# Gated delta rule with a routed feed-forward: the sums of squares of the output move to ScalarE's accumulator

## The chip, the core and the metric

The kernel runs on one core of a Trainium2 chip, as one launch. The metric is the device time in microseconds (us). The kernel before takes 2626.98 us, the median of three runs (2621.15 to 2629.7). Below, PE is TensorE, DVE is VectorE, ACT is ScalarE, POOL is GpSimd, and SP is the engine that only issues transfers.

## What is computed

The reference adds three things: the input x, a routed feed-forward of layernorm(x) (the best 2 of 8 experts for each token), and an attention of the gated delta rule on layernorm(x). There are 4 sequences of 2048 tokens, 256 channels, 8 heads, keys of 128 and values of 64. Cut to the part that matters here, all in float32:

```python
def step(S, inp):                       # over the tokens of a sequence
    q_t, k_t, v_t, g_t, b_t = inp
    S = S * jnp.exp(g_t)[..., None, None]
    u = (v_t - jnp.einsum('bhk,bhkv->bhv', k_t, S)) * b_t[..., None]
    S = S + jnp.einsum('bhk,bhv->bhkv', k_t, u)
    o_t = jnp.einsum('bhk,bhkv->bhv', q_t, S)
    return (S, o_t)
...
o = gated_delta_rule(q, k, v, g, beta)
gv = (x @ Wg).reshape(Bx, Tx, H, DV)
o = o * lax.rsqrt(jnp.mean(o * o, axis=-1, keepdims=True) + EPS) * norm_w
o = o * jax.nn.silu(gv)
return o.reshape(Bx, Tx, H * DV) @ Wo
```

The change is about `jnp.mean(o * o, axis=-1)`: for each token and head, the sum of the squares of 64 numbers.

## The kernel before, in words

There are three stages, one after the other: `norm_and_route` (layernorm, routing), `experts` (the feed-forward) and `attention`. Only `attention` is changed. Every engine runs its own list of instructions, written out in the program by hand, strictly in that order; semaphores (`wait(engine, name, count)`, `then_inc`) connect the lists. There is no scheduler, so an instruction that waits holds up all that stands behind it on its engine.

`attention` handles the 4 sequences side by side as 4 lanes of 32 partitions. The 2048 tokens of a sequence are 16 groups (the variable m) of 4 chunks (c) of 32 tokens. So a chunk is 128 rows, 32 tokens of each lane, and there are 64 chunks in all. For each group an engine runs two pieces:

- `scan(m, par, f)`: the four chunks of group m in order. With S the state of all heads, a chunk is this chain: PE `read_keys` (keys times S), DVE `read` (scales it into `ks`) and `residual` (`R`), PE `solve`, ACT `spread` (copies the result into `W`), PE `apply_state` in two halves, and DVE `apply_state` in two halves, which writes the new S. Only then can the next chunk's `read_keys` begin. Beside the chain PE makes `read_queries` and `apply_scores`, ACT copies them into `t2` (`read`), DVE adds them into the chunk's output `O` (`apply_scores`, L1670). Then comes the norm of the output: POOL squares it (`squares`, L1889, into `osq`, which is the same memory as `ks`), DVE sums 64 squares per head (`squares_sum`, L1690, into `ss`), POOL makes the factor (`factor`, L1896 and L1899: an addition and a power -1/2), and DVE scales by the factor and by the gate in the next chunk's list (`scale_out`, L1695 and L1699). PE turns the result (`turn`, L1233) and ACT copies it out (`turn`, L1452 into `oT`).
- `after_keys(f, ...)`: everything of the next group f = m + 1 that must be there before its scan: the projections and short convolutions of its values and queries, and on DVE `invert`, a chain of 69 small dependent steps that inverts the 32x32 triangles.

The keys of the next group are made inside the scan of this one, one pair of heads for each chunk: PE `project_head(f, c, h)`, ACT `tap3_head(f, c, h)` (a small copy into `tails`, L1366, and the first product of the convolution into `cv`, L1369), DVE `head_taps` (a small correction, L1543, which waits for `tap3_done`, and three taps, L1548), and ACT `silu(f, other, c)` (L1381 into `kT`), after which `cv` goes on. In the scan of ACT the order in a chunk is: `tap3_head(f, c, 0)`, `spread`, `tokens`, `tap3_head(f, c, 1)`, in chunk 0 `decays` (an exponential, with a table load), `read`, `tokens`, `turn(m, c - 1)`, `silu(f, other, c)`. In chunk 0 of a group with a next one a second table load stands ahead of `silu`. In the scan of DVE it is: `read`, `residual`, the correction of the next keys, taps with `expert_rows` and `scale_out(m, c - 1)` between them, `apply_state(m, c, 0)`, and after more taps `apply_state(m, c, 1)` and `squares_sum(m, c)`; in chunk 3 `squares_sum` stands ahead of `apply_state(m, c, 1)`. In after_keys PE begins with `keys(f, par, 0)`, which needs `silu(f, other, 3)`, and DVE begins `invert` after its two products L1600, the second of which needs `keys(f, par, 1)`.

The functions that are changed, and those that call them:

Of the kernel before, what the change touches and what calls it, by code (L numbers as in the profile page):

```python
# [12 lines left out]
ALU = mybir.AluOpType  # L13
# [6 lines left out]
P = 128  # L20
# [819 lines left out]
def attention(nc, keep, dims, loaded_params, NPARAM, xf, xnT_d, yg_d, stat_d, of):  # L840
# [11 lines left out]
    with ExitStack() as ctx:  # L852
        def sb(name, shape, dt=F32):
# [15 lines left out]
        Y = sb("Y", [P, U, CT]); AT = sb("AT", [P, 2, U, CT])  # L869
        lanes = sb("lanes", [P, CT, CT]); lane_t = sb("lane_t", [P, 256]); vr = sb("vr", [P, GROUP, HV]); ktok = sb("ktok", [P, 2, H, P])  # L870
        S = sb("S", [P, LANES, HV]); Sd = sb("Sd", [P, LANES, HV])
        ks = sb("ks", [P, HV])[:, :]; osq = ks
        R = sb("R", [P, HV]); W = sb("W", [P, H, 2, DV]); in_pair = sb("in_pair", [P, 2])
        t2 = sb("t2", [P, HV]); O = sb("O", [P, HV]); O3 = sb("O3", [P, HV])
        ss = sb("ss", [P, H]); f1 = sb("f1", [P, H]); fo = sb("fo", [P, H])
# [9 lines left out]
        names = {  # L885
            "tensor": "proj_ready gate_ready norms_mm dexp_ready kk_ready qk_ready vtr_ready ktok_ready "
                      "ks_ready s_read w_ready aw_ready sup_ready otr_ready wo_ready",
            "scalar": "tap3_done tails_done silu_done sq_ready gate_done dec_done ktok_done w_spread t2_done oT_done vr_done",
            "vector": "tap taps_done norm_read nq_done nk_done kk_used qk_used elim "
                      "ks_scaled r_done o_sum s_half s_done ss_done o2_done o3_done acc1_done acc2_done fin_done",  # L890
            "gpsimd": "wt_done sidx_done k_halo_step k_halo vq_halo_step vq_halo qg_ready knorm_done "
                      "sd_half sd_done osq_done f_step f_done",
        }
        s = {n: ctx.enter_context(nc.semaphore("att_" + n)) for group in names.values() for n in group.split()}
        consts = ctx.enter_context(nc.semaphore("att_consts"))
# [68 lines left out]
        def heads(ap):  # L964

            return ap.rearrange("p (h v) -> p h v", h=H)
# [375 lines left out]
        def _(act):  # L1342
# [80 lines left out]
            def read(m, par, c):  # L1423
# [5 lines left out]
                    last = A(t2[:, DV * h:DV * h + DV], pC[:, 1, DV * h:DV * h + DV], ACT.Copy, scale=mst[:, par, c, 2, h:h + 1])  # L1429
                last.then_inc(s["t2_done"], 1)  # L1430

            def spread(m, c):

                n = GROUP * m + c
                wait(act, "w_ready", n + 1)
                for two in range(2):
                    wait(act, "sup_ready", 2 * n - 1 + two)
                    if two == 0:
                        wait(act, "aw_ready", n)
                    hs = slice(4 * two, 4 * two + 4)  # L1440
                    for k in range(2):
                        last = A(W[:, hs, k, :], heads(pC[:, 0, :])[:, hs, :], ACT.Copy, scale=in_pair[:, k:k + 1])  # L1442
                    last.then_inc(s["w_spread"], 1)
# [55 lines left out]
            def scan(m, par, f):  # L1499
                more = f is not None  # L1500
                other = 1 - par
                for c in range(GROUP):
                    if c == 0:
                        read(m, par, 0)
                    if more:
                        tap3_head(f, c, 0)
                    spread(m, c)
                    if c in (1, 2):
                        tokens(m, par, c + 1, 0)
                    if more:  # L1510
                        tap3_head(f, c, 1)
                    if more and c == 0:
                        decays(f, other, 0)
                    if c:
                        read(m, par, c)
                    if c in (1, 2):
                        tokens(m, par, c + 1, 1)
                    if c:
                        turn(m, c - 1)
                    if more:  # L1520
                        silu(f, other, c)
                    if more and c == 3:
                        decays(f, other, 1)
                if more:
                    after_keys(f, other, m)
                else:
                    turn(m, 3)
# [4 lines left out]
        def _(dve):  # L1532
# [108 lines left out]
            def read(m, par, c):  # L1641
                n = GROUP * m + c
                wait(dve, "ks_ready", n + 1)
                wait(dve, "ss_done", n)
                dve.wait_ge(mst_loaded, 16 * m + 16)
                wait(dve, "r_done", n)
                V.tensor_tensor(heads(ks), heads(pC[:, 0, :]), bc(mst[:, par, c, 2, :], 2, DV), op=ALU.mult).then_inc(s["ks_scaled"], 1)
# [33 lines left out]
            def expert_rows_2(m, c):  # L1681
                n = GROUP * m + c
                wait(dve, "acc1_done", n + 1)
                V.scalar_tensor_tensor(out=xr[:, c, :], in0=yb[:, c, 1, :], scalar=wt[:, c, 1:2], in1=xr[:, c, :], op0=ALU.mult, op1=ALU.add).then_inc(s["acc2_done"], 1)

            def squares_sum(m, c):
                n = GROUP * m + c
                wait(dve, "osq_done", n + 1)
                wait(dve, "f_done", n)
                V.tensor_reduce(ss[:, :], heads(osq), op=ALU.add, axis=AX_X).then_inc(s["ss_done"], 1)  # L1690

            def scale_out(m, c):
                n = GROUP * m + c
# [55 lines left out]
            def scan(m, par, f):  # L1749
                more = f is not None  # L1750
                for c in range(GROUP):
# [29 lines left out]
                        pass  # L1781
                    for _ in fill_late:
                        pass
                    if c == 3:
                        squares_sum(m, c)
                    apply_state(m, c, 1)
                    if c < 3:
                        squares_sum(m, c)
                    if c == 3:
                        expert_rows(m, c)  # L1790
                        expert_rows_2(m, c)
# [10 lines left out]
        def _(pool):  # L1802
# [79 lines left out]
                G.tensor_tensor(new, old, bc(mst[:, par, c, 4:4 + LANES, hs], 3, DV),  # L1882
                                op=ALU.mult).then_inc(s["sd_done" if two else "sd_half"], 1)

            def squares(m, c):
                n = GROUP * m + c
                wait(G, "o_sum", n + 1)
                wait(G, "ss_done", n)
                G.tensor_tensor(osq, O[:, :], O[:, :], op=ALU.mult).then_inc(s["osq_done"], 1)  # L1889

            def factor(m, c):

                n = GROUP * m + c
# [20 lines left out]
            def scan(m, par, f, last):  # L1914
                more = f is not None
                for c in range(GROUP):
                    if more and c == 0:
                        decay_sums(f, 1 - par, 0)
                    if c < 3:
                        read(m, par, c + 1, 0)  # L1920
                    squares(m, c)
                    if more and c == 2:
                        decay_sums(f, 1 - par, 1)
                    if c < 3:
# [36 lines left out]
```

## Time and profile before

| | |
|---|---|
| median of three runs | 2626.98 us |
| the profiled execution | 2646.84 us, of it the span 2645.2 us |
| busy, share of the span | PE 82%, DVE 72%, ACT 49%, POOL 42% |
| the granted clock of PE, mean over the span | 0.978 of full speed |
| a group of the attention, 1011 to 1116 us | PE 91.39, DVE 96.12, ACT 64.73, POOL 45.51 us busy of 105 |

The span begins with routing and experts (about 830 us, in which PE reaches 9 tenths only in the experts) and goes on with the attention's groups, each some 105 to 110 us long: about 48 us of scan and 57 us of after_keys. A timeline row gives the start and the duration in us, the engine (PEld is PE's loading of weights), the line, the operation, what is written from what, the shapes, and in brackets the idle time of the engine before it with what ended it. Small numbers can overlap: on one engine an instruction may start about 0.1 us before the one ahead of it is done. A group of rows of the view by line gives count, busy time, mean duration of one, and the idle time before them.

### The profile page before, as it was taken

The numbers are of one execution on the slowest core, as the hardware profiler recorded it, in microseconds if no ns is written. First come the engines' busy times: TensorE is split into PE (matmuls) and PEld (weight loads), VectorE is DVE, ScalarE is ACT, GpSimd is POOL, SyncE is SP. The second block draws the span as 40 slices with busy tenths as digits, with TensorE's granted clock in tenths as the row PEclk, the third lists the DMA queues.
The fourth block names the chain that finished last, engine by engine and source line by source line (L and its number), as shares of the span: only waits on it lengthen the run. The fifth ranks groups of instructions, "written<-read, shape, count | busy, mean of one in ns | idle before, by whom it ended". The sixth has DMA issues, their size and how long they took to land. (4 is left out here: it accounts for less than half of the span.)

```text
span 2645.2 us, 93006 instructions
## 1 busy us (share of the span) xinstructions
PE 2173.0 (82%) x36317; PEld 1501.1 (57%) x36318; DVE 1896.5 (72%) x3928; ACT 1302.6 (49%) x3667; POOL 1120.0 (42%) x1123
## 2 busy tenths in 40 slices
PE   3222399999997798988989889898888988989886
PEld 2222399999995364555645546455464555645555
DVE  5343352223222789998898998989989999899985
ACT  0000144444433656566565665656656566565662
POOL 3444344444443242634426344263442634526333
PEclk9999999999998899999999999999999999999998
DMA  6445122222222101001010010100101001010000
GB/s 200 155 154 182 49 71 70 70 75 72 74 70 76 35 4 44 22 25 31 16 43 23 25 32 15 44 23 25 32 15 44 23 25 33 15 44 23 25 22 23
DMA packets 106778, 135.23 MB, mean 51 GB/s; under 512 B 39584, under 2 KB 80064, under 8 KB 106176
## 3 DMA queue, kind: packets, MB, share of 16 engines
q0 software_dynamic: 23296, 60.85, 7.4%
q1 hardware_dynamic: 65952, 48.91, 6.7%
q10 hardware_dynamic: 17184, 20.49, 2.3%
q8 instruction: 261, 4.28, 0.7%
q14 instruction: 85, 0.70, 0.1%
HBM read 76.18 MB, written 54.00 MB: 49 GB/s over the span
## 5 line engine op out<-in xcount | busy, mean ns | idle before, releaser
L1548 DVE SCALAR_TENSOR_TENSOR att_cv<-att_psA,att_cw,att_cv 128x508 f32<-128x508 f32 (+2 forms) x660 | 480.0, 739 | 7.6
L1085 PE MATMUL att_psA<-att_xt,att_wqkv 128*128 128x512 f32 x880 | 445.1, 640 | 14.1 <-DMA att_xt<-xn_cols 12.7
L1882 POOL TENSOR_TENSOR att_Sd<-att_S,att_mst 128x1024 f32<-128x1024 f32 x128 | 242.9, 1903 | 461.7 <-DVE att_S L1662 438.6
L807 PE MATMUL moe_psHT<-moe_xT,moe_w1s 128*128 128x128 f32 x2176 | 268.0, 277 | 0.3 <-issue 0.3
L1085 PEld LDWEIGHTS att_psA<-att_xt,att_wqkv 128*128 128x128 f32 x880 | 161.1, 199 | 184.0 <-issue 167.7
L817 PE MATMUL moe_psY<-moe_w,moe_hT 128*128 x1088 | 258.1, 380 | 0.0
L807 PEld LDWEIGHTS moe_psHT<-moe_xT,moe_w1s 128*128 128x128 f32 x2176 | 256.1, 193 | 0.9 <-issue 0.5
L672 ACT ACTIVATE moe_hT<-moe_psHT,moe_b1T 128x128 f32<-128x128 f32 x544 | 156.0, 369 | 200.5 <-PE moe_psHT L807 199.2
L771 DVE TENSOR_TENSOR moe_y<-moe_psY,moe_b2b 128x256 f32<-128x256 f32 x136 | 57.8, 425 | 254.5 <-PE moe_psY L817 154.1
L1548 DVE SCALAR_TENSOR_TENSOR att_cv<-att_psC,att_cw,att_cv 128x508 f32<-128x508 f32 (+2 forms) x300 | 215.0, 738 | 0.6
L817 PEld LDWEIGHTS moe_psY<-moe_w,moe_hT 128*128 128x128 f32 x1088 | 197.1, 191 | 21.4
L1868 POOL TENSOR_TENSOR att_qg<-tri_q,att_mst 128x512 f32<-128x512 f32 x32 | 34.8, 1087 | 387.0 <-DMA att_mst<-token_stats 378.1
L1085 PE MATMUL att_psC<-att_xt,att_wqkv 128*128 128x512 f32 x400 | 192.6, 618 | 7.2 <-DVE att_cv L1548 5.2
L635 POOL DMA_DIRECT2D expert_out<-moe_y x136 | 98.0, 720 | 237.4 <-DVE moe_y L771 216.4
L265 POOL DMA_INDIRECT slot_tokens<-route_token,route_where x128 | 124.1, 969 | 167.7 <-DVE route_where L373 129.2
L763 DVE COPY moe_w1s<-moe_w 128x1024 f32 x136 | 94.7, 697 | 114.5 <-issue 91.8
L1429 ACT ACTIVATE att_t<-att_psC,att_mst 128x64 f32<-128x64 f32 x512 | 114.8, 380 | 115.4 <-PE att_psC L1179 115.4
L1662 DVE TENSOR_TENSOR att_S<-att_psS,att_Sd 128x1024 f32<-128x1024 f32 x128 | 155.8, 1217 | 19.8 <-PE att_psS L1210 19.6
L1634 DVE TENSOR_TENSOR att_lanes<-att_lanes,att_lane_t 128x30 f32<-128x30 f32 (+14 forms) x480 | 160.4, 334 | 8.3
L1632 DVE TENSOR_TENSOR att_lane_t<-att_lanes 128x30 f32<-128x30 f32 (+14 forms) x480 | 160.0, 333 | 7.2
L1442 ACT ACTIVATE att_W<-att_psC,att_in_pair 128x256 f32<-128x256 f32 x256 | 100.9, 481 | 130.5 <-PE att_psC L1191 130.5
L629 POOL DMA_INDIRECT moe_xt<-xn_rows,moe_ids x136 | 133.8, 984 | 65.7 <-issue 45.6
(238 smaller groups left out, 4331.6 us busy)
## 6 DMA issues: line engine op xcount, KB each, us to landing
expert_out<-moe_y POOLq DMA_DIRECT2D x136, 128.0 KB
route_x_in<-in_L_attn_x_dram SPq DMA_DIRECT2D x64, 128.0 KB
moe_w<-in_L_ffn_W_dram SPq DMA_DIRECT2D x16, 512.0 KB
xn_rows<-route_xn ACTq DMA_DIRECT2D x16, 512.0 KB
xn_cols<-route_xnT ACTq DMA_DIRECT2D x16, 512.0 KB
att_xt<-xn_cols SPq DMA_DIRECT2D x16, 512.0 KB, 4.4
att_xr<-in_L_attn_x_dram SPq DMA_DIRECT2D x64, 128.0 KB, 2.7
out_dram<-att_xr SPq DMA_DIRECT2D x256, 32.0 KB
```

Of the source, the lines that this page charges most:

```text
L265: pool.indirect_dma_start(ids_d[:, :], bass.IndirectOffsetOnAxis(ap=where[:, t, k:k + 1], axis=0), token[:, t:t + WIDE], None).then_inc(sc ...
L629: pool.indirect_dma_start(xt[:, par], None, xn_d[:, :], bass.IndirectOffsetOnAxis(ap=ids[:, par, 0:1], axis=0)).then_inc(x_loaded[par], 16)
L672: last = nc.scalar.activation(hT[:, par, c], psHT[par][:, c * P:(c + 1) * P], ACT.Relu, bias=b1T[:, bass.ds(e * HC + c, 1)])
L807: last = nc.tensor.matmul(psHT[par][:, c * P:(c + 1) * P], w1s[:, par, d, c * P:(c + 1) * P], xT[:, par, d], start=(d == 0), stop=(d == DC ...
L817: last = nc.tensor.matmul(psY[par][:, 0:D], hT[:, par, c], w2[:, bass.ds(e, 1), c].rearrange("p o n -> p (o n)"), start=(c == 0), stop=(c ...
L1085: last = MM(pair_bank(m, j)[:, h, :], wqkv[:, c, (2 * j + h) * P:(2 * j + h + 1) * P], xt[:, c, :], start=(c == 0), stop=(c == DC - 1))
L1429: last = A(t2[:, DV * h:DV * h + DV], pC[:, 1, DV * h:DV * h + DV], ACT.Copy, scale=mst[:, par, c, 2, h:h + 1])
L1548: last = V.scalar_tensor_tensor(out=late, in0=by_lane(pair_bank(m, j)[:, h, :])[:, :, 0:LT - d], scalar=cw[:, 2 * j + h, TAPS - 1 - d:TAPS ...
L1632: link(V.tensor_tensor(tmp, lanes[:, j + 1:32, j:j + 1].to_broadcast([P, 31 - j, j]), lanes[:, j:j + 1, 0:j].to_broadcast([P, 31 - j, j]), ...
L1634: link(V.tensor_tensor(lanes[:, j + 1:32, 0:j], lanes[:, j + 1:32, 0:j], tmp, op=ALU.add))
L1662: V.tensor_tensor(new, pS[:, :, :].rearrange("p b (l x) -> p (b l) x", l=2), old, op=ALU.add).then_inc(s["s_done" if two else "s_half"], 1)
L1882: G.tensor_tensor(new, old, bc(mst[:, par, c, 4:4 + LANES, hs], 3, DV), op=ALU.mult).then_inc(s["sd_done" if two else "sd_half"], 1)
```

## The change

`osq` becomes a tile of its own. POOL's `squares` and DVE's `squares_sum` are removed, with their calls and the two semaphore counts that tied `ks` to `osq`. ACT gets a `squares_sum`: for each of the 8 heads one `Square` activation of 128x64 that also writes the sum along its row into one column of `ss` (`accum_out`). It waits for `o_sum` (the chunk's output is there) and for `f_done` of the chunk before, and is called after `turn(m, c - 1)` and ahead of `silu(f, other, c)`.

```diff
-        ks = sb("ks", [P, HV])[:, :]; osq = ks
+        ks = sb("ks", [P, HV])[:, :]; osq = sb("osq", [P, HV])
...
+            def squares_sum(m, c):
+
+                n = GROUP * m + c
+                wait(act, "o_sum", n + 1)
+                wait(act, "f_done", n)
+                for h in range(H):
+                    hs = slice(DV * h, DV * h + DV)
+                    last = A(osq[:, hs], O[:, hs], ACT.Square, accum_out=ss[:, h:h + 1])
+                last.then_inc(s["ss_done"], 1)
...
                     if c:
                         turn(m, c - 1)
+                    squares_sum(m, c)
                     if more:
                         silu(f, other, c)
...
             def read(m, par, c):
                 n = GROUP * m + c
                 wait(dve, "ks_ready", n + 1)
-                wait(dve, "ss_done", n)
...
-            def squares_sum(m, c):
-                n = GROUP * m + c
-                wait(dve, "osq_done", n + 1)
-                wait(dve, "f_done", n)
-                V.tensor_reduce(ss[:, :], heads(osq), op=ALU.add, axis=AX_X).then_inc(s["ss_done"], 1)
...
-                    if c == 3:
-                        squares_sum(m, c)
                     apply_state(m, c, 1)
-                    if c < 3:
-                        squares_sum(m, c)
...
-            def squares(m, c):
-                n = GROUP * m + c
-                wait(G, "o_sum", n + 1)
-                wait(G, "ss_done", n)
-                G.tensor_tensor(osq, O[:, :], O[:, :], op=ALU.mult).then_inc(s["osq_done"], 1)
...
                     if c < 3:
                         read(m, par, c + 1, 0)
-                    squares(m, c)
```

ACT around the end of chunk 1 and the start of chunk 2, before (`att_oT` is `turn`, `att_kT` is `silu`, `att_tails` with `att_cv` is `tap3_head` of the next chunk, `att_W` is its `spread`):

```order
L1429 ACTIVATE att_t<-att_psC,att_mst 128x64 x8
L1409 ACTIVATE att_ktok<-att_psB,att_mst 128x128 x4
L1452 ACTIVATE att_oT<-att_psC 128x512
L1381 ACTIVATE att_kT<-att_cv 128x4x4x32 x2
L1366 ACTIVATE att_tails<-att_psA 128x12
L1369 ACTIVATE att_cv<-att_psA,att_cw 128x512
L1442 ACTIVATE att_W<-att_psC,att_in_pair 128x4x64 x4
```

The same place after:

```order
L1429 ACTIVATE att_t<-att_psC,att_mst 128x64 x8
L1409 ACTIVATE att_ktok<-att_psB,att_mst 128x128 x4
L1462 ACTIVATE att_oT<-att_psC 128x512
L1439 ACTIVATE att_osq,att_ss<-att_O 128x64 x8
L1381 ACTIVATE att_kT<-att_cv 128x4x4x32 x2
L1366 ACTIVATE att_tails<-att_psA 128x12
L1369 ACTIVATE att_cv<-att_psA,att_cw 128x512
L1452 ACTIVATE att_W<-att_psC,att_in_pair 128x4x64 x4
```

Eight activations now stand ahead of `silu` and of the next chunk's `tap3_head` and `spread`. Line numbers behind the new function are ten higher.

DVE at the same time, before (from the second half of the state to the next chunk's correction):

```order
L1662 TENSOR_TENSOR att_S<-att_psS,att_Sd 128x4x256
L1690 TENSOR_REDUCE att_ss<-att_ks 128x8
L1647 TENSOR_TENSOR att_ks<-att_psC,att_mst 128x512
L1654 TENSOR_TENSOR att_R<-att_vr,att_ks 128x512
L1543 TENSOR_TENSOR att_cv<-att_cv,att_corr 128x4x3
```

The reduction L1690 goes; nothing else moves on DVE in chunks 0 to 2.

## Rows read from the trace of the kernel before

**Rows 1.** The page: busy time of each engine over the span.
```profile
PE 2173.0 (82%) x36317; PEld 1501.1 (57%) x36318; DVE 1896.5 (72%) x3928; ACT 1302.6 (49%) x3667; POOL 1120.0 (42%) x1123
```
**Rows 2.** By stretch: PE, PEld, DVE, ACT, POOL (count), clock, DMA; a group, the last scan.
```profile
1011.00:1116.00 105.00, 91.39 (x1951) 57.25 (x1950) 96.12 (x189) 64.73 (x180) 45.51 (x42) 1.00 0.09 25
2586.00:2629.00 43.00, 33.49 (x1071) 28.57 (x1068) 28.96 (x41) 19.13 (x67) 22.68 (x18) 0.96 0.08 21
```
**Rows 3.** Timeline, PE and DVE, from chunk 1's sum to chunk 3's read.
```profile
1179.36 0.68 DVE L1690 TENSOR_REDUCE att_ss<-att_ks 128x8 f32<-128x512 f32 x1
1179.50 1.10 PE L1168 MATMUL att_psC<-att_S,att_kT 128*32 128x64 f32 x64 [0.47 <-DVE att_S L1662]
1180.67 0.69 DVE L1647 TENSOR_TENSOR att_ks<-att_psC,att_mst 128x512 f32<-128x512 f32 x1 [0.63 <-PE att_psC L1168]
...
1182.06 0.16 DVE L1543 TENSOR_TENSOR att_cv<-att_cv,att_corr 128x12 f32<-128x12 f32 x1
...
1193.07 0.69 DVE L1647 TENSOR_TENSOR att_ks<-att_psC,att_mst 128x512 f32<-128x512 f32 x1 [0.63 <-PE att_psC L1168]
```
**Rows 4.** Timeline, ACT, the same stretch and what stands around it.
```profile
1174.30 1.82 ACT L1429 ACTIVATE att_t<-att_psC,att_mst 128x64 f32<-128x64 f32 x8
...
1179.07 0.60 ACT L1452 ACTIVATE att_oT<-att_psC 128x512 f32<-128x512 f32 x1 [1.93 <-PE att_psC L1233]
1179.57 1.15 ACT L1381 ACTIVATE att_kT<-att_cv 128x512 f32<-128x512 f32 x2
1180.61 0.17 ACT L1366 ACTIVATE att_tails<-att_psA 128x12 f32<-128x12 f32 x1
1180.67 0.69 ACT L1369 ACTIVATE att_cv<-att_psA,att_cw 128x512 f32<-128x512 f32 x1
1183.61 1.57 ACT L1442 ACTIVATE att_W<-att_psC,att_in_pair 128x256 f32<-128x256 f32 x4 [2.25 <-PE att_psC L1191]
```
**Rows 5.** By line, 1000 to 2640 us: removed instructions and nearest kin of the added.
```profile
L1690 DVE TENSOR_REDUCE att_ss<-att_ks 128x8 f32<-128x512 f32 x60 | 40.6, 677 | 1.8 <-POOL att_ks L1889 1.8
L1889 POOL TENSOR_TENSOR att_ks<-att_O 128x512 f32<-128x512 f32 x60 | 62.4, 1040 | 75.7 <-DVE att_O L1670 75.7
L1429 ACT ACTIVATE att_t<-att_psC,att_mst 128x64 f32<-128x64 f32 x480 | 107.6, 380 | 108.9 <-PE att_psC L1179 108.9
L1388 ACT ACTIVATE att_sq<-att_qT 128x1024 f32<-128x1024 f32 x60 | 63.6, 1060 | 1.0
```
**Rows 6.** Timeline, DVE and ACT, chunk 0 to chunk 1.
```profile
1163.81 0.68 DVE L1670 TENSOR_TENSOR att_O<-att_psC,att_t 128x512 f32<-128x512 f32 x1
...
1166.02 1.28 ACT L1381 ACT_TABLE_LOAD   x1 [2.25 <-DVE att_cv L1548]
...
1168.43 0.68 ACT L1369 ACTIVATE att_cv<-att_psA,att_cw 128x512 f32<-128x512 f32 x1
...
1169.66 0.16 DVE L1543 TENSOR_TENSOR att_cv<-att_cv,att_corr 128x12 f32<-128x12 f32 x1
```
**Rows 7.** Timeline, ACT, PE and DVE, chunk 3 and the start of after_keys.
```profile
1201.28 0.60 ACT L1452 ACTIVATE att_oT<-att_psC 128x512 f32<-128x512 f32 x1 [1.40 <-PE att_psC L1233]
1202.26 1.15 ACT L1381 ACTIVATE att_kT<-att_cv 128x512 f32<-128x512 f32 x2 [0.39 <-DVE att_cv L1548]
...
1203.46 1.30 PE L1128 MATMUL att_psA<-att_kT 128*32 128x32 f32 x128 [1.15 <-ACT att_kT L1381]
...
1208.00 0.69 DVE L1600 TENSOR_TENSOR att_Y<-att_psA,att_AT 128x512 f32<-128x512 f32 x1 [1.13 <-PE att_psA L1128]
```
**Rows 8.** Timeline, POOL, the factor of chunk 3.
```profile
1202.90 0.20 POOL L1896 TENSOR_TENSOR att_f<-att_ss,att_nq 128x8 f32<-128x8 f32 x1 [0.98 <-DVE att_ss L1690]
1203.18 1.64 POOL L1899 TENSOR_TENSOR att_fo<-att_f,att_mhalf 128x8 f32<-128x8 f32 x1
```
**Rows 9.** Timeline, PE: one operation at either clock, 64 instructions each.
```profile
1171.66 1.10 PE L1179 MATMUL att_psC<-att_S,att_qT 128*32 128x64 f32 x64
2584.08 1.93 PE L1179 MATMUL att_psC<-att_S,att_qT 128*32 128x64 f32 x64
```

More of the change, by code:

```diff
@@ L887, in attention @@
                       "ks_ready s_read w_ready aw_ready sup_ready otr_ready wo_ready",
-            "scalar": "tap3_done tails_done silu_done sq_ready gate_done dec_done ktok_done w_spread t2_done oT_done vr_done",
+            "scalar": "tap3_done tails_done silu_done sq_ready gate_done dec_done ktok_done w_spread t2_done oT_done vr_done ss_done",
             "vector": "tap taps_done norm_read nq_done nk_done kk_used qk_used elim "
-                      "ks_scaled r_done o_sum s_half s_done ss_done o2_done o3_done acc1_done acc2_done fin_done",
+                      "ks_scaled r_done o_sum s_half s_done o2_done o3_done acc1_done acc2_done fin_done",
             "gpsimd": "wt_done sidx_done k_halo_step k_halo vq_halo_step vq_halo qg_ready knorm_done "
-                      "sd_half sd_done osq_done f_step f_done",
+                      "sd_half sd_done f_step f_done",
         }
```

## The prediction

> **What bounds the kernel now.** The page's first part gives the usual suspicion: PE is busy for 82% of the span and DVE for 72%, ACT for 49% [rows 1]. The share over the span hides the stages, so the view by stretches comes next. In one group of the attention DVE is busy for 96.12 of 105 us and PE for 91.39, ACT for 64.73 and POOL for 45.51 [rows 2]. PE and DVE are both nearly full there, at a granted clock of 1.00, and ACT has a third to spare. A third to spare does not say where, so the timelines of one chunk decide.
>
> PE's read of the keys for chunk 2 was waiting for the state, starts at 1179.50 and takes 1.10; DVE's `ks` starts at 1180.67, having been idle for 0.63 although the reduction L1690 stood in that same gap [rows 3]. The next `ks` follows 12.40 later and again shows 0.63 of idle time, and DVE's rows between the two show no other wait: apart from that 0.63 DVE's list is full from one `ks` to the next, and the new state is part of it. Whatever holds DVE up at the correction (L1543, 1182.06) moves the next state by the same amount. That correction needs ACT's `cv`, which is ready at 1180.67 + 0.69 = 1181.36 [rows 4]: a slack of 0.70 us. ACT itself goes without a pause from `turn` (`oT`, 1179.07) through `silu` to `cv`. Its idle time lies before `turn` (1.93) and after `cv` (2.25, ended by PE) [rows 4], and the new work stands between `turn` and `silu`, where ACT has none.
>
> **What is removed.** From DVE 64 reductions of 0.677 us, from POOL 64 squares of 1.040 us [rows 5]. Summed up, DVE would win 43 us. But in chunks 0 to 2 the reduction lies beside PE's read of the keys: without it the idle time before `ks` grows from 0.63 to about 1.3 and `ks` starts when it did [rows 3]. I value this at nothing; its cover is PE's 1.10, which doesn't go. In chunk 3 the reduction stands ahead of the state, but what comes next is decided by ACT and PE: PE's `keys` waited 1.15 for ACT's `silu` and DVE's second product L1600 waited 1.13 for PE [rows 7]. Again nothing. POOL's squares are off the path: POOL waits for the output, 75.7 us over the 60 [rows 5]. The freed wait on `ks` was met long before `ks` ran. A separate `osq` costs no time.
>
> **What is added.** Call X the time ACT spends on the eight squares of a chunk. No row has an activation with an accumulator, so X is bounded.
> - The same shape, 128x64 from PSUM with a scale per row, takes 0.380 us alone [rows 5], but eight in a row take 1.82 [rows 4], so one starts every 0.2: 0.22 if the last is counted whole as well.
> - Low end: `Square` of 1024 columns takes 1.060 [rows 5]. A 512-column copy (`oT`) takes 0.60 [rows 4], so a column costs about 0.9 ns, 64 columns make about 0.19, and with the 0.1 by which neighbours overlap (`oT` ends at 1179.67, `silu` starts at 1179.57 [rows 4]) one starts every 0.1: X = 0.8, if giving out the sum is free.
> - High end: each activation runs to its end, 0.38, and giving out the sum is a further small instruction that overlaps nothing, 0.17 like the 128x12 one [rows 4]: 8 x 0.55 = 4.4.
> - I take 0.22 for the activation, the row of its own shape, and 0.08 for giving out the sum, about the step by which the 128x12 copy moves its successor (1180.61 to 1180.67 is 0.06 [rows 4]): X = 8 x 0.30 = 2.4.
>
> A time below nothing is excluded: ACT did none of this before.
>
> On the length of an activation the row shows 1.060 us for a `Square` of 1024 columns [rows 5]. The Trainium skill ("ScalarE: Activation LUTs", section "What ACT_TABLE_LOAD costs") gives 186 ns + 0.833 ns a column for an activation with immediate operands, and neighbours that overlap by 93 ns. That makes 1.039 for this row, so the trace agrees within 2%, and for 64 columns 0.146 from start to start, an estimate of 1.2 us for eight; no price for giving out the sum stands there. By it the sum below would be 26 us instead of 87. The same page (section "Rules for kernel authors") says to do a plain multiplication on VectorE rather than ScalarE. That speaks against this change, and the timeline bears it out only as far as the place goes: ACT is the engine without slack just there.
>
> **What it costs, transition by transition.** The rest of ACT's list shifts by X, less what it waited for anyway.
> - Chunk 1 to 2: `cv` is ready at 1181.36 + X, DVE wants it at 1182.06. DVE stalls for X - 0.70 = 1.70 [rows 3, 4]. Queued behind the stalled correction on DVE are the taps, the expert rows, `scale_out` and the half of the state, so PE's second `apply_state`, the next projection and `turn` all follow. ACT's `spread` of chunk 2 would start at 1183.76 instead of 1183.61, which the later DVE hides.
> - Chunk 2 to 3: the same, 1.70.
> - Chunk 0 to 1: the squares can start when the output is there, 1163.81 + 0.68 = 1164.49, and end at 1166.89. The table load ahead of `silu` started at 1166.02, so it comes 0.87 later; `cv` was ready at 1169.11 for a correction at 1169.66, a slack of 0.55 [rows 6]. Stall: 0.32, in general X - 2.08. The order shows no further table load, so there is no term for one.
> - Chunk 3 to after_keys: `turn` ends at 1201.88, the squares at 1204.28, and `silu` starts there instead of at 1202.26. PE's `keys` follow directly, and DVE's L1600 after them [rows 7]: X - 0.38 = 2.02. The factor on POOL needs 0.20 and 1.64 [rows 8], so it is there at about 1206.2, and `scale_out` (two of some 0.7, as `ks` in rows 3) ends at 1207.6, ahead of PE's second `keys`, now 1210.0: hidden. The inversion and all of after_keys begin with that L1600 and with PE's `keys`, so they move as a whole; I see nothing there that takes the delay back.
>
> Sum for a group: 0.32 + 1.70 + 1.70 + 2.02 = 5.74 us, or 4X - 3.86. It occurs in the 15 scans that make keys for a next group. In the last scan there is no `silu` and no `cv`; ACT is busy for 19.13 of 43 us [rows 2] and has room, and I put nothing for it beyond some tenths at the very end. 15 x 5.74 = 86 us. The durations are those of the profiled execution, 2646.84 us (span 2645.2), which lies 0.75% above the median of the runs; the sum is carried to the median unchanged: 2627 + 86 = 2713 us. At X = 0.8 it is 15 x (0.10 + 0.10 + 0.42) = 9 us, 2636; at X = 4.4 it is 15 x 13.74 = 206 us, 2833.
>
> **The rivals.**
> - Giving out the sum is dear (X of 3.2 to 4.4). For it: nothing in the trace shows the operation. Against: small activations overlap well [rows 4]. At X = 3.6 the time is 2627 + 158 = 2785.
> - Giving out the sum is nearly free (X under 1.6). Chunk 0's term is gone then and a group costs 3X - 1.78: 2636 at X = 0.8, 2627 + 36 = 2663 at 1.4, 2672 at 1.6. For it: the low end of the estimate. Against: the row of the same shape starts one every 0.2.
> - Faster: DVE is what bounds the scan, so that each reduction taken away shortens it: 64 x 0.677 = 43 us, 2584 us, with the squares in ACT's idle third. For it: DVE busy 96 of 105 us. Against: the 0.63 of idle time before `ks`, ended by PE [rows 3], and the 1.93 of ACT's idle time lies on the wrong side. It decides only if X is below 0.7 and DVE wins somewhere I don't see.
> - PE's clock falls. PE gets 1.70 of idle time in a step that had little, and 1.15 + 2.02 = 3.2 at the start of after_keys. In the last scan, where PE works 33.49 of 43 us, the granted clock is 0.96 against 1.00 in the full group [rows 2], and the 64 matmuls of one read take 1.93 at the level of 1.2 GHz against 1.10 at 2.4 [rows 9]. If a stretch of each step is run so where PE decides, once or twice that 0.83 is added four times a group: 50 to 100 us more, 2763 to 2813. Against: 0.96 is little. (The skill, "TensorE: Matmul & The Clock Gate", says likewise that pauses of the engine bring the slower level.)
>
> **How the numbers follow.** My forecast (X of 1.6 to 3.2, 2672 to 2761) gets 0.62, the dear sum 0.15, the nearly free one 0.10 (a third of it near enough to nothing to count as no change), the clock 0.09, DVE's gain 0.04. A measurement of this kernel can tell about 0.3%, 8 us, from no change. Slower is then 0.92, no change 0.05, faster 0.03. The range of 8 in 10 leaves out the faster case, most of the nearly free one and the top of the dear one and of the clock: 2650 to 2795.
>
> **What would show it.** In the profile after: eight squares a chunk and how long they take together, which gives X; a new idle time of DVE before the correction L1543 of about X - 0.70 in chunks 2 and 3, ended by ACT's `cv`; 1.3 instead of 0.63 idle before `ks`; the distance from one `ks` to the next 12.40 + 1.7 in a scan; a later `silu` and a wait of about 3.2 before PE's `keys`; POOL idle for longer. It is wrong if DVE's stall appears but the group isn't longer (then after_keys takes it back), if the distance between two `ks` stays at 12.4, or if PE's granted clock in the scans is clearly below 1.00.

## The result, and the profile after

The changed kernel takes 2698.51 us (median of 4 runs, 2695.3 to 2721.29) where the kernel before takes 2628.29 (median of 4, 2621.15 to 2629.7): a ratio of 1.0291, with a 95% interval of 1.0231 to 1.0352. It is slower by 70 us. The forecast was slower by 86, at 2713 us with a range of 2650 to 2795.

The page's first part of the profile after stands against [rows 1]:

```profile
PE 2189.8 (81%) x36317; PEld 1512.7 (56%) x36318; DVE 1860.2 (69%) x3864; ACT 1421.1 (53%) x4691; POOL 1051.1 (39%) x1059
```

DVE lost 36 us of work, POOL 69 and ACT gained 118.5. PE, whose instructions are the same in number, is busy for 17 us longer; that is a first sign of its clock. ACT's instruction count grew by 1024, not by 512: each square with an accumulator leaves two records. By line, over 1000 to 2690 us (count, busy us, mean ns of one, idle time before them and what ended it):

```profile
L1439 ACT ACTIVATE att_osq<-att_O 128x64 f32<-128x64 f32 x480 | 115.0, 244 | 4.1 <-DVE att_O L1680 4.0
L1439 ACT ACTIVATION_READ_ACCUMULATOR att_osq<-att_O 128x1 f32 x480 | 91.2, 190 | 0.0
L1657 DVE TENSOR_TENSOR att_ks<-att_psC,att_mst 128x512 f32<-128x512 f32 x60 | 41.4, 690 | 62.2 <-PE att_psC L1168 62.2
```

The timeline of ACT in one chunk 1 gives their place and their price (start, length, engine, line, tile; in brackets the idle time before and what ended it):

```profile
1749.41 0.60 ACT L1462 ACTIVATE att_oT<-att_psC 128x512 f32<-128x512 f32 x1 [2.18 <-PE att_psC L1233]
1749.91 0.25 ACT L1439 ACTIVATE att_osq<-att_O 128x64 f32<-128x64 f32 x1
1750.05 0.19 ACT L1439 ACTIVATION_READ_ACCUMULATOR att_osq<-att_O 128x1 f32 x1
1750.15 0.24 ACT L1439 ACTIVATE att_osq<-att_O 128x64 f32<-128x64 f32 x1
...
1751.73 0.19 ACT L1439 ACTIVATION_READ_ACCUMULATOR att_osq<-att_O 128x1 f32 x1
1751.82 1.13 ACT L1381 ACTIVATE att_kT<-att_cv 128x512 f32<-128x512 f32 x2
1752.86 0.16 ACT L1366 ACTIVATE att_tails<-att_psA 128x12 f32<-128x12 f32 x1
1752.92 0.67 ACT L1369 ACTIVATE att_cv<-att_psA,att_cw 128x512 f32<-128x512 f32 x1
```

The squares start at 1749.91 and `silu` at 1751.82, so X, the time of eight squares with their sums, is 1.91 to 1.92 us, 0.24 for each. An activation moves what follows it by 0.146 (start to start), and the read-out of its sum, 0.190 long, by only 0.094. `oT` to `silu` was 0.50 before [rows 4] and is 2.41 now. ACT waits ahead of `turn` still, 2.18 us, where its new work does not stand.

DVE in the same stretch, and on to the next `ks`:

```profile
1750.95 0.69 DVE L1657 TENSOR_TENSOR att_ks<-att_psC,att_mst 128x512 f32<-128x512 f32 x1 [1.22 <-PE att_psC L1168]
1751.67 0.69 DVE L1664 TENSOR_TENSOR att_R<-att_vr,att_ks 128x512 f32<-128x512 f32 x1
1753.62 0.17 DVE L1554 TENSOR_TENSOR att_cv<-att_cv,att_corr 128x12 f32<-128x12 f32 x1 [1.26 <-ACT att_cv L1369]
...
1757.91 1.21 DVE L1672 TENSOR_TENSOR att_S<-att_psS,att_Sd 128x1024 f32<-128x1024 f32 x1
...
1761.92 1.21 DVE L1672 TENSOR_TENSOR att_S<-att_psS,att_Sd 128x1024 f32<-128x1024 f32 x1
1764.36 0.69 DVE L1657 TENSOR_TENSOR att_ks<-att_psC,att_mst 128x512 f32<-128x512 f32 x1 [1.22 <-PE att_psC L1168]
```

Two forecasts can be read off. The idle time before `ks` is 1.22 where it was 0.63 [rows 3]: the reduction went and left only a longer wait for PE. And there is a new stall of 1.26 before the correction, ended by ACT's `cv`. From one `ks` to the next it takes 13.41, against 12.40 [rows 3].

The end of the same group, from three timelines. PE:

```profile
1772.01 1.16 PE L1210 MATMUL att_psS<-att_W,att_ktok 64*128 64x128 f32 x16 [1.63 <-DVE att_S L1672]
...
1777.38 1.77 PE L1128 MATMUL att_psA<-att_kT 128*32 128x32 f32 x128 [2.55 <-ACT att_kT L1381]
1779.08 3.02 PE L1085 MATMUL att_psC<-att_xt,att_wqkv 128*128 128x512 f32 x4
```

ACT:

```profile
1773.79 0.60 ACT L1462 ACTIVATE att_oT<-att_psC 128x512 f32<-128x512 f32 x1 [2.64 <-PE att_psC L1233]
...
1776.20 1.14 ACT L1381 ACTIVATE att_kT<-att_cv 128x512 f32<-128x512 f32 x2
```

DVE:

```profile
1778.60 0.69 DVE L1699 TENSOR_TENSOR att_O<-att_O,att_fo 128x512 f32<-128x512 f32 x1 [1.81 <-POOL att_fo L1893]
...
1783.36 0.69 DVE L1611 TENSOR_TENSOR att_Y<-att_psA,att_AT 128x512 f32<-128x512 f32 x1 [2.75 <-PE att_psA L1128]
```

`silu` starts 2.41 after `oT` instead of 0.98 [rows 7]; PE's `keys` waits 2.55 for it instead of 1.15. That is 1.4, where the forecast had 2.02. The factor on POOL is late as well, but DVE then waits 2.75 for PE anyway: hidden, as forecast. What was not in the forecast's sum is the length of PE's rows. `keys` takes 1.77 instead of 1.30, and the projection's row behind it (two calls, which the profile counts as x4) takes 3.02. The same row in the kernel before:

```profile
1204.69 1.98 PE L1085 MATMUL att_psC<-att_xt,att_wqkv 128*128 128x512 f32 x4
```

The view by stretches has the reason in its granted clock (PE, PEld, DVE, ACT, POOL with counts, clock, DMA share, GB/s), first in the middle of the scan, then here:

```profile
1745.00:1765.00 20.00, 17.76 (x402) 12.33 (x403) 16.05 (x25) 14.53 (x69) 10.59 (x7) 1.00 0.01 3
1777.00:1784.00 7.00, 6.62 (x262) 4.46 (x263) 2.62 (x5) 2.21 (x3) 5.47 (x4) 0.76 0.02 5
```

After PE's pauses of 1.12, 1.63 and 2.55 us its clock stands at the lower of its two levels, 1.2 instead of 2.4 GHz, for part of that stretch. In 12 of 15 groups `keys` or the projection behind it is longer than in the kernel before (`keys` itself in 7 of them), and in 3 neither is. Count the slower stretches of the whole profile from 900 us on and there are 30, against 19 before.

To see where a group's time goes I cut it at events of DVE: from `ks` of chunk 0 to those of chunks 1, 2 and 3, from there to the second product `Y` of after_keys, and on to the next group's `ks`. Means in us over 14 groups:

| kernel | ks0 to ks1 | ks1 to ks2 | ks2 to ks3 | ks3 to Y | Y to next ks | group |
|---|---|---|---|---|---|---|
| before | 23.72 | 12.47 | 12.43 | 15.41 | 46.06 | 110.09 |
| after | 23.47 | 12.66 | 13.46 | 18.77 | 45.73 | 114.08 |

The group is 3.99 us longer, and 15 x 3.99 = 60. All of it lies between `ks` of chunk 1 and `Y`, 4.58 in sum; the two other parts win 0.58, for a reason that I did not look for. (The stall before a chunk's correction comes behind that chunk's `ks`, so what the squares of chunk 1 cost stands in the column ks2 to ks3, and what those of chunk 2 cost in ks3 to Y, together with chunk 3's.) The remaining 10 us between the medians are not located. The two profiled executions differ by 54.6 only: the first `ks` comes 6.8 us earlier in the one after (918.71 against 925.54), and the profiled execution of before, 2646.84, lies above all its timed runs.

### The profile page after: what moved, and what is told of

Same layout as the page of the kernel before. It is cut to its first block and busy times, and to the rows that moved or that the text cites. A ratio compares the mean times of both kernels' runs of the same rounds, so it can differ in the third digit from the quotient of the medians.

```text
span 2699.8 us, 93773 instructions
## 1 busy us (share of the span) xinstructions
PE 2189.8 (81%) x36317; PEld 1512.7 (56%) x36318; DVE 1860.2 (69%) x3864; ACT 1421.1 (53%) x4691; POOL 1051.1 (39%) x1059
## 5 line engine op out<-in xcount | busy, mean ns | idle before, releaser
L1085 PE MATMUL att_psC<-att_xt,att_wqkv 128*128 128x512 f32 x400 | 207.4, 658 | 7.3 <-DVE att_cv L1559 5.3
L1210 PE MATMUL att_psS<-att_W,att_ktok 64*128 64x128 f32 x2048 | 152.3, 285 | 44.8 <-DVE att_S L1672 42.1
L1210 PEld LDWEIGHTS att_psS<-att_W,att_ktok 64*128 64x128 f32 x2048 | 128.0, 188 | 85.2 <-issue 75.0
```

Of the source, the lines that this page charges most:

```text
L1085: last = MM(pair_bank(m, j)[:, h, :], wqkv[:, c, (2 * j + h) * P:(2 * j + h + 1) * P], xt[:, c, :], start=(c == 0), stop=(c == DC - 1))
L1210: last = MM(pS[:, b, :].rearrange("p (l h v) -> p l h v", l=2, h=4)[:, :, h % 4, :], ktok[r, c % 2, h, :], W[r, h, :, :], start=True, stop ...
```

## The experiments

They ran on three chips. On two of them the kernel before takes 2531 us instead of 2628. It was not profiled there, but the kernel of relief, which takes the same time, was: its steps inside the scans are those of before (12.39 from one `ks` to the next, median), and its first `ks` comes at 826 us instead of 926, so the 100 us lie ahead of the attention. Every kernel is compared with the kernel before on its own chip. On such a chip the changed kernel took 2602.3 against 2530.71, 1.0283 (1.0267 to 1.0298): +71.6. Its group is 113.59 there, 4.40 over relief's 109.19, and `keys` or the projection is slow in 14 of 15 groups.

> The changed kernel itself, so that the others of this group and those before it, which were made on a chip where before takes 2531 us, have it beside them. Its theories expect 62 to 72 us over before, as on the first chip.

**relief.** The eight squares become one small activation; the sums are left out.

```
-                for h in range(H):
-                    ...
-                    last = A(osq[:, hs], O[:, hs], ACT.Square, accum_out=ss[:, h:h + 1])
-                last.then_inc(s["ss_done"], 1)
+                A(ss[:, :], O[:, 0:H], ACT.Square).then_inc(s["ss_done"], 1)
```

> The changed kernel with ScalarE's eight squares of a chunk replaced by one activation of 8 columns, so the sums of squares are left out (the output is not the reference's); VectorE's reductions and GpSimd's squares stay removed. X, the time ScalarE spends there, is then some 0.15 us. Theory (what is removed was hidden behind TensorE's read of the keys and behind ScalarE's silu): the time of before within 0.3%, 2620 to 2636 us, ks to ks 12.4 us, 1.2 us of idle time before ks. Rival (VectorE's list bounds the scan, each reduction taken away counts): 43 us faster than before, about 2585 us.

Measured: 2530.36 against 2530.92, 0.9999 (0.9989 to 1.001). DVE and POOL are rid of their work, ACT has almost none of it, and nothing is won. By line:

```profile
L1654 DVE TENSOR_TENSOR att_ks<-att_psC,att_mst 128x512 f32<-128x512 f32 x56 | 38.6, 690 | 51.3 <-PE att_psC L1168 51.3
```

51.3 / 56 = 0.92 us of idle time before each `ks`, and 1.22 in chunks 1 to 3 as in the changed kernel (chunk 0's has none here): the freed time has become a wait for PE. The rival of 43 us gained is ruled out. This kernel's group (109.19) is also the base for the kernels of these two chips.

**double.** Each square and sum is made twice, the second into tiles that nobody reads.

```
+                    A(osq2[:, hs], O[:, hs], ACT.Square, accum_out=ss2[:, h:h + 1])
                     last = A(osq[:, hs], O[:, hs], ACT.Square, accum_out=ss[:, h:h + 1])
```

> The changed kernel with each square and sum made twice (the second into tiles of its own that nothing reads): X = 3.84 us. Theory: terms X - 2.08 before chunk 1, X - 0.70 before chunks 2 and 3 (0.2 of each given back), X - 0.38 at the keys: 1.76 + 2.94 + 2.94 + 3.46 = 11.1 us a group, 166 us over before, and with a slower TensorE clock in the longer pauses up to 230. Rival (cost in proportion to X): twice that of the changed kernel, 125 to 144 us over.

Measured: 2751.26, 1.0871 (1.0857 to 1.0886), +220.5, three times the +71.6. So the slack ahead of the stall exists: twice X costs more than twice as much. DVE:

```profile
1848.89 0.69 DVE L1659 TENSOR_TENSOR att_ks<-att_psC,att_mst 128x512 f32<-128x512 f32 x1 [1.22 <-PE att_psC L1169]
1849.61 0.69 DVE L1666 TENSOR_TENSOR att_R<-att_vr,att_ks 128x512 f32<-128x512 f32 x1
1853.46 0.17 DVE L1556 TENSOR_TENSOR att_cv<-att_cv,att_corr 128x12 f32<-128x12 f32 x1 [3.16 <-ACT att_cv L1370]
```

The stall grew by 1.90, which is X's growth. And ks1 to ks2 is now 14.36 instead of 12.59 (medians), 1.77 more: the forecast's X - 2.08 for the step from chunk 0 to chunk 1, with X = 3.84, is 1.76. The whole is 48 us above 15 x (4X - 3.86) = 172. From 900 us on there are 54 stretches of PE's slower clock, against 26 in the changed kernel on this chip, and `keys` is slow in all 15 groups.

**no_sum.** The squares without the accumulator; `ss` is set once, so the sums are left out.

```
-                    last = A(osq[:, hs], O[:, hs], ACT.Square, accum_out=ss[:, h:h + 1])
+                    last = A(osq[:, hs], O[:, hs], ACT.Square)
```

> The changed kernel with the eight squares but without accum_out: the sums are left out (ss is set once, so the output is not the reference's). Theory (the cost is X less the slack): X falls from 1.92 to about 8 x 0.146 = 1.2 us; VectorE's stalls are 0.5 each in chunks 2 and 3, silu at the keys is 0.8 late: 1.4 to 1.8 us a group, 20 to 35 us over before. Rival (the activations' count costs, giving out the sum is free): as the changed kernel, 62 to 72 us over.

Measured: 2549.68, 1.0079 (1.0065 to 1.0092), +19. Eight bare activations take 1.15, which leaves 0.77 for eight read-outs. The stall is 0.39 in chunk 2 and 0.47 in chunk 3 (medians), and X - 0.70 = 0.45. The read-out is 40% of X but 53 of the 72 us. By the formula 35 of them are there because what comes first uses up the slack: 15 x 3.98 against 15 x 1.67. The other 18 fit the clock: PE's wait before `keys` is 1.81 here, and behind it `keys` and the projection are at 1.30 and 1.98 in all 15 groups.

**chunk3_old and only_chunk3.** In the first, chunk 3 alone is made the old way; in the second, chunks 0 to 2 are, and ACT makes chunk 3's.

```
# chunk3_old, ScalarE
-                    squares_sum(m, c)
+                    if c < 3:
+                        squares_sum(m, c)
# only_chunk3, ScalarE
-                    squares_sum(m, c)
+                    if c == 3:
+                        squares_sum(m, c)
```

> The changed kernel, but in chunk 3 of each group the squares and sums are made as before (GpSimd and VectorE); in chunks 0 to 2 ScalarE makes them behind turn. Theory: the part of chunk 3 is the silu that comes 1.54 us later, and TensorE's slower clock at the keys (12 of 15 groups, 1.5 us), some 2.7 us a group; left are the two stalls of VectorE at the correction in chunks 2 and 3, 1.0 net each: 30 us over before, about 2658 us. Rival (each chunk's squares cost alike, by their count): three quarters of 70 us, about 2681 us.

> The counterpart of the run with chunk 3 as before: here ScalarE makes squares and sums in chunk 3 alone, and chunks 0 to 2 are as before (GpSimd and VectorE). Theory (the parts add up): 72 us less the 31 of chunks 0 to 2 leaves about 40 us over before: the silu 1.5 us late in 15 groups, 23 us, and the slower TensorE clock there, up to 18. Rival (chunk 3 is expensive only because chunks 0 to 2 come before it): 23 us or less.

Measured: chunk3_old 2561.97, 1.0126 (1.0109 to 1.0143), +31; only_chunk3 2665.66 against 2631.43, 1.0139 (1.0117 to 1.0161), +34. Together 65 of 71.6: two costs of about the same size that nearly add up. With chunk 3 alone the group's other steps are those of before (12.52 and 12.41), and ks3 to Y is 17.52. PE's wait before `keys` is 2.55 again, and `keys` or the projection is slow in 10 of 15 groups; in chunk3_old the wait is 1.15 and none is slow.

**ahead_of_turn.** The call moves by one place on ACT, from behind `turn` to the idle time ahead of it.

```
+                    squares_sum(m, c)
                     if c:
                         turn(m, c - 1)
-                    squares_sum(m, c)
```

> The changed kernel with one call moved: the squares stand ahead of ScalarE's turn, in the 1.9 us for which it waits there, instead of behind it. The same work on every engine. Theory (the place is what costs, not the work): chunks 1 and 2 cost nothing, ks to ks is 12.4 us again and VectorE has no stall at the correction; in chunk 3 the squares run from the output at about 1.1 us before turn's old end, so silu comes about 1.0 us later: 15 x 1.0 = 15 us, with a slower TensorE clock at the keys up to 20 more: 2635 to 2665 us. Rival (ScalarE has too much work for the chunk, wherever it stands): the time of the changed kernel, about 2698 us.

Measured: 2547.35, 1.0059 (1.0045 to 1.0072), +16 instead of +72 with the same work on the same engine. ACT:

```profile
1761.93 0.19 ACT L1439 ACTIVATION_READ_ACCUMULATOR att_osq<-att_O 128x1 f32 x1
1762.44 0.60 ACT L1462 ACTIVATE att_oT<-att_psC 128x512 f32<-128x512 f32 x1 [0.32 <-PE att_psC L1233]
...
1771.60 0.26 ACT L1439 ACTIVATE att_osq<-att_O 128x64 f32<-128x64 f32 x1 [0.97 <-DVE att_O L1680]
...
1773.52 0.57 ACT L1462 ACTIVATE att_oT<-att_psC 128x512 f32<-128x512 f32 x1
1774.00 1.14 ACT L1381 ACTIVATE att_kT<-att_cv 128x512 f32<-128x512 f32 x2
```

In chunks 1 and 2 the squares are over 0.32 before `oT` can start. In chunk 3 they are not: `oT` follows without a wait, and PE's `keys` is late by what sticks out. First the same group, then an earlier one:

```profile
1775.19 1.30 PE L1128 MATMUL att_psA<-att_kT 128*32 128x32 f32 x128 [1.95 <-ACT att_kT L1381]
```

```profile
1108.09 1.62 PE L1128 MATMUL att_psA<-att_kT 128*32 128x32 f32 x128 [2.11 <-ACT att_kT L1381]
1109.64 3.21 PE L1085 MATMUL att_psC<-att_xt,att_wqkv 128*128 128x512 f32 x4
```

The wait is 2.11 or 2.12 in 14 of the 15 groups; 1.95 is the exception. 2.11 - 1.15 = 0.96 a group is 14 of the 16 us. The slower clock is rarer than in the changed kernel but not gone: `keys` or the projection is slow in 7 of 15 groups. This profiled execution is the slowest of the kernel's six runs (2558.96), so the profile shows more of that than the median has.

**ahead_chunk3_old.** Both edits: ahead of `turn` in chunks 0 to 2, the old way in chunk 3.

> ScalarE's squares ahead of turn in chunks 0 to 2, chunk 3 as before. Both places at which the changed kernel pays are gone. Theory: before's time within 0.3% (within 8 us), ks to ks 12.4. Rival (16 us of the run ahead of turn are not chunk 3's, but ScalarE's work): some 12 us over before.

Measured: 2634.52 against 2631.43, 1.0011 (0.9998 to 1.0025): no difference that can be told. With both places of the loss mended the loss is gone, and nothing is gained for it.

**pe_filled and pe_filled_less.** Matmuls that nobody needs fill PE's wait before `keys`, four in the first kernel, two in the second.

```
+                        wait(pe, "o_sum", GROUP * (m + 1))
+                        for i in range(2):
+                            MM(pC[:, 0, :], ident[:, :], wqkv[:, 0, 0:512], start=True, stop=True)
```

> The changed kernel with four more matmuls of 512 columns (2.0 us at full clock, into a free bank, their result is not used) in the 2.55 us for which TensorE waits ahead of the keys of the next group. Theory with the clock: the keys take 1.30 instead of 1.77 us and the projection behind them 1.98 instead of 3.02, in 12 of 15 groups: 18 us less than the changed kernel, about 2680 us. Rival (the slower matmuls there are hidden by VectorE, or the clock doesn't come from that pause): 2698 us, and if the added matmuls delay the keys, more.

> As the filled kernel, with two more matmuls (1.8 us) instead of four, which turned out to take 3.6 us and to hold up the keys by 0.85 us. Theory with the clock: the keys no longer wait for the added ones, and they and the projection run at full clock: 0.85 x 15 = 13 us less than with four, that is some 50 us over before, against 62 to 72 for the changed kernel. Rival (the slower clock there costs nothing): no less than the changed kernel.

Measured: pe_filled 2594.52 against 2530.92, 1.0246 (1.0232 to 1.026), +63.6; pe_filled_less 2584.37, 1.0218 (1.0199 to 1.0237), +53.7. PE with four, then with two:

```profile
1792.98 3.60 PE L1334 MATMUL att_psC<-att_wqkv,ident 128*128 128x512 f32 x8
1796.50 1.30 PE L1128 MATMUL att_psA<-att_kT 128*32 128x32 f32 x128
1797.73 1.98 PE L1085 MATMUL att_psC<-att_xt,att_wqkv 128*128 128x512 f32 x4
```

```profile
1784.86 1.88 PE L1334 MATMUL att_psC<-att_wqkv,ident 128*128 128x512 f32 x4
1787.57 1.30 PE L1128 MATMUL att_psA<-att_kT 128*32 128x32 f32 x128 [0.83 <-ACT att_kT L1384]
```

Four were a mistake of mine in size: they take 3.60 us, longer than the wait, and hold `keys` up, so their time says little. (A call of 512 columns is counted as two, x8 for the four, and takes 0.90.) Their rows already say that `keys` is back at 1.30 and the projection at 1.98. Two leave 0.83 of the wait, so they delay nothing, and the kernel is 2602.3 - 2584.4 = 18 us faster than the changed one although PE does more. `keys` takes 1.30 and the projection 1.98 or less in all 15 groups, and ks3 to Y falls from 18.94 to 17.83 in the mean, which is 17 of the 18 us. Those 18 us are the clock's.

**tap_in_gap and before_tap_moved.** If DVE now has 1.2 us free before `ks`, something can be put there: in chunks 0 to 2 the last tap of DVE's convolution moves from ahead of the second half of the state to behind it. The first kernel is ahead_chunk3_old with that edit, the second is the kernel before with it.

```
-                    for _ in fill_late:
-                        pass
                     if c == 3:
+                        for _ in fill_late:
+                            pass
                         ...
+                    next(fill_late, None)
                     apply_state(m, c, 1)
+                    for _ in fill_late:
+                        pass
```

> As the last one, and in chunks 0 to 2 VectorE's last tap of the next keys stands behind the second half of the state, in the 1.2 us for which VectorE waits for TensorE since the reduction is gone. The state is then ready 0.7 us earlier. Theory: VectorE's list would allow 11.7 us from ks to ks, TensorE's, which has 0.4 to 0.5 us of idle time in a chunk, about 12.0: 0.3 to 0.4 less in three steps of 15 groups, 10 to 25 us faster than before. Rival (TensorE or ScalarE bounds the step already): no gain.

> The kernel before with the same tap moved behind the second half of the state in chunks 0 to 2, its squares and sums untouched on GpSimd and VectorE. Theory: behind the state stand then a tap of 0.73 and a reduction of 0.68, 0.2 more than the 1.22 us until the keys' read is done; ks is 0.2 late, but the state 0.7 early, so ks to ks is 11.9 to 12.0: nearly the same gain, 8 to 25 us faster than before, and the change itself isn't needed for it. Rival (only without the reduction is there room): less than 5 us.

Measured: tap_in_gap 2624.68, 0.9974 (0.9958 to 0.999), -7; before_tap_moved 2626.46, 0.9981 (0.9964 to 0.9998), -5. Both gain less than I expected (10 and 8 us at least). tap_in_gap beats the kernel before by a little, and against ahead_chunk3_old it wins 9.8 us. DVE:

```profile
1825.74 0.69 DVE L1658 TENSOR_TENSOR att_ks<-att_psC,att_mst 128x512 f32<-128x512 f32 x1 [0.88 <-PE att_psC L1168]
...
1834.90 1.21 DVE L1673 TENSOR_TENSOR att_S<-att_psS,att_Sd 128x1024 f32<-128x1024 f32 x1
1836.04 0.73 DVE L1560 SCALAR_TENSOR_TENSOR att_cv<-att_psA,att_cw,att_cv 128x500 f32<-128x500 f32 x1
1837.58 0.69 DVE L1658 TENSOR_TENSOR att_ks<-att_psC,att_mst 128x512 f32<-128x512 f32 x1 [0.82 <-PE att_psC L1168]
...
1379.86 0.49 DVE L1555 TENSOR_TENSOR att_cv<-att_cv,att_corr 128x12 f32<-128x12 f32 x1 [0.71 <-ACT att_cv L1369]
```

The tap stands in the gap, and that step takes 11.84 instead of 12.40. In the mean ks2 to ks3 fell by 0.49, but ks1 to ks2 rose by 0.16, and ks3 to Y did not move. The last row, from chunk 1 of another group, shows why no more came of it: the `silu` behind chunk 0's tap starts later, `cv` with it, and DVE stalls at the correction again (0.81 in the mean; in chunks 2 and 3 it does not). It is the same thin slack on ACT. By the same edit the kernel before gains 5.0, with its reduction still there. The runs of these kernels spread over 12 to 20 us, so that 9.8 and 5.0 are hardly told apart, and against the kernel before the two come out alike (-7 and -5): the change isn't needed for this gain.

## Why the prediction was right, and where its sizes were off

Its mechanism was right. Taken by its own steps:

- **The removed work is worth nothing.** Right: relief shows 0.9999, and the idle time before `ks` became 1.22 (forecast 1.3).
- **X.** The term that was mis-sized: 2.4 forecast, 1.92 measured. The read-out was nearly right (0.08 forecast, 0.094 measured). The activation was not: 0.22 forecast, 0.146 measured. I took the row of the same shape, but that row reads PSUM and scales by a tile, which a square of an SBUF tile does not; the shape was the weaker likeness. My low end, 0.10 from the 1024- and 512-column activations, was too short by about as much. The Trainium skill ("ScalarE: Activation LUTs", section "What ACT_TABLE_LOAD costs") gave 186 ns + 0.833 ns a column, less 93 of overlap, which for 64 columns is 239 ns long and 0.146 from start to start; the trace has 244 and 0.146, so it agrees. It has no price for the read-out.
- **Chunk 0 to 1.** X - 2.08 is below nothing for 1.92, so no stall, and none is there. double confirms the slack. The step ks1 to ks2 still grew by 0.19. It has two DVE rows that are longer than their like one chunk on:

```profile
1741.75 0.67 DVE L1694 SCALAR_TENSOR_TENSOR att_xr<-att_yb,att_wt,att_xr 128x256 f32<-128x256 f32 x1
1742.33 0.88 DVE L1699 TENSOR_TENSOR att_O<-att_O,att_fo 128x512 f32<-128x512 f32 x1
```

  One chunk on they take 0.48 and 0.68. POOL works beside them here, but it does so in the kernel before as well, where they take 0.48 and 0.69 and one of POOL's small products (`ctmp`, 96 columns) takes 1.20 in most groups. In the changed kernel that product takes 0.36. So in these kernels either POOL's row or DVE's is long, and no run tests why it changed sides.
- **Chunks 1 to 2 and 2 to 3.** X - 0.70 = 1.22; the stall is 1.26. But `ks` moved by only 1.01. The forecast read DVE's rows between two `ks` as having no other wait, and that was wrong: 0.25 is given back within the step. In the kernel before the two halves of the state lie 4.29 apart, 4.01 after, since DVE waited there for ACT's `t`:

```profile
1186.34 1.22 DVE L1662 TENSOR_TENSOR att_S<-att_psS,att_Sd 128x1024 f32<-128x1024 f32 x1
...
1188.60 0.69 DVE L1670 TENSOR_TENSOR att_O<-att_psC,att_t 128x512 f32<-128x512 f32 x1 [0.19 <-ACT att_t L1429]
...
1190.63 1.22 DVE L1662 TENSOR_TENSOR att_S<-att_psS,att_Sd 128x1024 f32<-128x1024 f32 x1
```

  A later DVE finds `t` ready. That small wait was a slack, and it stood in the trace to be read.
- **Chunk 3 to after_keys.** X - 0.38 = 1.54; the wait for `silu` grew by 1.40. The factor on POOL was hidden, as said.
- **The clock.** Set apart as a rival at 0.09 and left out of the sum, with 50 to 100 us for it. It came, in another place than the mid-scan reads on which I priced it: `keys` and the projection behind the longest wait, in 12 to 14 groups of 15, worth 18 us by pe_filled_less. I weighed it as something that happens or doesn't; it was a small term of the sum. The granted clock of 0.96 in a stretch with pauses [rows 2] was the hint.

By the forecast's formula with the measured X a group costs 0 + 1.22 + 1.22 + 1.54 = 3.98 us, and 15 groups 60. With the clock's 18 it is 78. What is given back (0.25 in each of two steps, and the 0.58 of the group's other parts) takes 16 off and the longer step ks1 to ks2 adds 3, which leaves 65. The profiled groups show 60 and, on the second chip, 66; the medians differ by 70 and 72, and where those last us lie is open. So it was partly luck that the forecast of 86 came so close: two errors, X too large by 26 us (15 x (5.74 - 3.98)) and the clock left out with 18, went against each other. (The forecast names its sum as 87 in one place; 15 x 5.74 is 86.)

## What to carry to other kernels

An engine's idle share doesn't say whether it can take more work: what counts is the slack between the place where the new work stands in its list and the next thing that another engine takes from it. The same eight squares cost 72 us behind `turn`, 16 ahead of it, and nothing that can be told ahead of it with chunk 3 left out. And work removed next to a wait for another engine only lengthens the wait. To win by it, something has to be moved into the gap, and here the slack of the same engine bounds that as well.

## What the runs showed of the hardware

- A `Square` with `accum_out` is two instructions on ACT: the activation (128x64, 0.244 us) and an ACTIVATION_READ_ACCUMULATOR (0.190) that starts 0.14 to 0.15 behind it and moves the next by 0.094. Reading durations alone one would have 0.43 for the pair; in a row it costs 0.24.
- `Square` brought no table load: the profile has 67 before and after. The one ahead of `silu` in chunk 0 comes later, behind the squares, and as long as before (1.28):

```profile
1736.50 0.19 ACT L1439 ACTIVATION_READ_ACCUMULATOR att_osq<-att_O 128x1 f32 x1
1736.71 1.28 ACT L1381 ACT_TABLE_LOAD   x1
```

- PE's clock can fall in a kernel in which PE is busy for most of the scan (17.76 of 20 us in its middle). What differs between the kernels is PE's wait before `keys`. Groups of 15 in which `keys` or the projection behind it took longer than its 1.30 or 1.98:

| kernel | PE's wait before `keys`, us | groups with slow rows |
|---|---|---|
| before, relief, chunk3_old | 1.15 | 0 |
| no_sum | 1.81 | 0 |
| ahead_of_turn | 2.11 | 7 |
| only_chunk3 | 2.55 | 10 |
| after, changed_again | 2.55 (in after 1.50 in one group) | 12, 14 |
| double | 3.40 | 15 |

  Matmuls of 1.88 us that nobody needs, put into the wait of 2.55, kept the level at 2.4 GHz in all 15 (pe_filled_less). The shorter pauses ahead of the long one, as the 1.12 and 1.63 in the group shown, are not needed for it: in only_chunk3 they are 0.3 to 0.6.
